# Row sums on ScalarE in place of VectorE's batch-norm statistics, in an attention and feed-forward kernel with hand-written orders

## The reference, cut to what matters

```
q   = layernorm(x)                      # over the 256 positions, eps 1e-5
kv  = k_i * v_j  (all channel pairs of a head, each position)
y   = causal convolution of kv with ssm_kernel[head]  + kv * D[head]
x   = x + sum_i y_ij * q_i
f   = layernorm(x)
x   = x + down( silu(gate(f)) * up(f) ) # HID = 704, weights are integers
```

## Time and profile before

| | |
|---|---|
| device time, median of 3 runs | 77.92 us (77.67 to 78.04) |
| span of the profiled execution, first to last instruction | 76.7 us |
| PE busy | 70.7 us, 92% |
| DVE busy | 63.9 us, 83% |
| POOL busy | 54.6 us, 71% |
| ACT busy | 46.7 us, 61% |
| chain that ended last, shares | PE 58%, DMA 15%, DVE 14%, ACT 3% |

### The profile page before, as it was taken

One profiled execution on the slowest core, in us unless ns is written; L12 is line 12 of the kernel. 1 busy time (PEld: TensorE's weight loads), 2 busy tenths in 40 slices (PEclk: granted clock), 3 DMA queues, 4 the chain that ended last, 5 costly groups with the idle time before them and its releaser, 6 DMA issues.

```text
span 76.7 us, 1495 instructions
## 1 busy us (share of the span) xinstructions
PE 70.7 (92%) x469; PEld 57.8 (75%) x469; DVE 63.9 (83%) x191; ACT 46.7 (61%) x115; POOL 54.6 (71%) x73
## 2 busy tenths in 40 slices
PE   4999988879999999999999999999999999999920
PEld 3767735568798777787888797988897989899810
DVE  0088399969999999899999999999999993786760
ACT  0601483275859587976868468746767798766400
POOL 5004798799889599299899949459627899939230
PEclk9999999999999999999999999999999999999995
DMA  0498999999997000000000000000000222200404
GB/s 5 132 256 279 386 344 295 285 384 397 386 353 220 13 0 0 0 0 4 4 9 0 0 0 0 0 0 0 0 9 4 68 68 68 68 9 0 137 0 137
DMA packets 7304, 8.29 MB, mean 108 GB/s; under 512 B 992, under 2 KB 6400, under 8 KB 7296
## 3 DMA queue, kind: packets, MB, share of 16 engines
q1 hardware_dynamic: 6912, 8.00, 31.7%
q10 hardware_dynamic: 384, 0.19, 0.8%
HBM read 7.12 MB, written 1.07 MB: 107 GB/s over the span
## 4 chain that ended last, share of the span: by engine, by line
PE 58%; DMA 15%; DVE 14%; SPq 3%; ACT 3%; issue 2%; DVEq 0%; ACTq 0%
PE conv L1010 18%; PE turn L957 8%; PE down L1029 8%; DMA k_ext<-ctx_ext 8%; DMA toeplitz<-taps 7%; PE conv L977 6%; PE conv L988 6%; PE conv L986 6%; DVE hidden L733 3%; DVE terms L718 2%; PE turn L939 2%; DVE terms L721 2%; PE turn L1029 2%; SPq L310 2%; ACT gate_act L508 1%
## 5 line engine op out<-in xcount | busy, mean ns | idle before, releaser
L1010 PE MATMUL conv<-f_parts,wgu 128*128 128x256 f16 x176 | 21.6, 273 | 0.3
L1010 PEld LDWEIGHTS conv<-f_parts,wgu 128*128 128x128 f16 x176 | 16.7, 98 | 3.5 <-DVE hidden L733 0.8
L376 POOL TENSOR_TENSOR products<-k_ext 128x512 f32<-128x512 f32 (+1 forms) x16 | 18.0, 1144 | 0.6 <-DMA k_ext<-ctx_ext 0.6
L508 ACT ACTIVATE gate_act<-conv,sg_sb 128x256 f32<-128x256 f32 (+1 forms) x24 | 11.2, 471 | 4.6 <-PE conv L1010 4.0
L258 POOL TENSOR_TENSOR h_lo<-hidden,h_hi 128x256 fp32r<-128x256 f32 x18 | 12.9, 729 | 1.4 <-ACT h_hi L513 1.3
L733 DVE SCALAR_TENSOR_TENSOR hidden<-conv,su_sb,gate_act 128x256 f32<-128x256 f32 (+1 forms) x24 | 11.3, 479 | 3.1 <-ACT gate_act L508 2.7
L977 PE MATMUL conv<-products,toeplitz 128*128 128x288 f32 x32 | 11.2, 434 | 0.3 <-DVE terms L725 0.3
L365 POOL TENSOR_TENSOR rstd_f<-variance_f,minus_half 128x1 f32<-128x1 f32 x8 | 5.5, 683 | 7.9 <-DVE variance_f L694 7.9
L718 DVE TENSOR_TENSOR terms<-conv,q_ext 128x512 f32<-128x512 f32 x16 | 10.8, 678 | 0.0
L986 PE MATMUL conv<-products,toeplitz 128*128 128x288 f32 x32 | 10.8, 422 | 0.0
L988 PE MATMUL conv<-products,toeplitz 128*128 128x288 f32 x32 | 10.4, 406 | 0.0
(11 more groups left out here) (64 smaller groups left out, 119.8 us busy)
## 6 DMA issues: line engine op xcount, KB each, us to landing
k_ext<-ctx_ext SPq DMA_DIRECT2D x3, 384.0 KB, 6.1
toeplitz<-taps_pad SPq DMA_DIRECT2D x2, 512.0 KB, 7.9
out<-x_sb SPq DMA_DIRECT2D x8, 128.0 KB, 1.7
toeplitz<-taps SPq DMA_DIRECT2D x3, 256.0 KB, 5.3
wg_int<-wg_t SPq DMA_DIRECT2D x1, 704.0 KB, 8.2
wu_int<-wu_t SPq DMA_DIRECT2D x1, 704.0 KB, 9.5
wd_int<-wd_t SPq DMA_DIRECT2D x1, 640.0 KB, 8.6
x_sb<-x SPq DMA_DIRECT2D x1, 512.0 KB, 7.0
```

The source lines that it names most:

```text
L376: nc.gpsimd.tensor_tensor(view(products[:, n:n + 1], first * MADE + GROUP, [[MADE, halves], [GROUP, 4], [1, GROUP]]), view(k, 0, [[EXT * B ...
L508: nc.scalar.activation(gate_act[up_lanes(t), i % 2, t, :], gate_of(i, t), ACT.Silu, scale=sg_sb[gate_lanes(t), t:t + 1]).then_inc(gate_act ...
L1010: done = nc.tensor.matmul(bank_of(i, t)[:, n, :], wgu[:, c, column:column + P], f_parts[:, i % 2, part, c, :], start=(c == 0 and part == 0 ...
```

## The change

For tiles 2 to 7, `stats_of_q` and `moments_of_q` on DVE go. ACT instead makes two passes over a tile's rows: `center_q` copies them scaled by -1/256 with the row sum in the accumulator output, which gives minus the mean; `spread_of_q` squares the rows plus that value, again with the row sum, which gives 256 times the variance. Their element-wise outputs go to `scratch`, which nobody reads. DVE turns two tiles' sums into variances in one operation (`variance_of_q_pair`), and POOL takes the power of both in one (`root_q_pair`), so that tiles 2/3, 4/5 and 6/7 share one of each. The shift multiplies minus the mean with the root.

The transfer of `skip` to all partitions goes: its 16 values stand in front of k's in DRAM and come with the first transfer of k. The small transfer of `skip_sb` goes too: D stands in the unused first column of `taps`. ACT issues two transfers where it issued four.

The four lists of POOL, ACT, DVE and PE are laid out anew over their whole length; SP's list keeps its order. The diff below is cut to the functions and to the lists' first part; behind it, operations of all kinds change places by a few positions.

```diff
+VECTOR_STATS = 2
...
-def build(nc, x, ctx_ext, taps, skip, wg_t, s_gate, wu_t, s_up, wd_t, s_down, taps_pad, out):
+def build(nc, x, ctx_skip, taps, wg_t, s_gate, wu_t, s_up, wd_t, s_down, taps_pad, out):
...
-k_ext = sb("k_ext", [P, H, HALVES, EXT * B])
+k_skip = sb("k_skip", [P, H + H * HALVES * EXT * B])
+skip_all = k_skip[:, 0:H]
+k_ext = k_skip[:, H:].rearrange("p (h c n) -> p h c n", h=H, c=HALVES)
...
-skip_sb = sb("skip_sb", [H, 1])
-skip_all = sb("skip_all", [P, H])
...
-minus_half = sb("minus_half", [P, 1])
+minus_half = sb("minus_half", [P, 2])
...
+minus_mean_q = sb("minus_mean_q", [P, TILES])
+spread_q = sb("spread_q", [P, TILES])
+scratch = sb("scratch", [P, 2, TILES, L])
...
     def load_k(first, last, done):
-        sp.dma_start(k_ext[:, first:last], ctx_ext[:, first:last]).then_inc(done, 16)
+        row = HALVES * EXT * B
+        columns = slice(H + first * row if first else 0, H + last * row)
+        sp.dma_start(k_skip[:, columns], ctx_skip[:, columns]).then_inc(done, 16)

...
     def root_q(t):
         wait(pool, q_variance, t + 1)
-        nc.gpsimd.tensor_tensor(rstd_q[:, t:t + 1], variance_q[:, t:t + 1], minus_half[:, :],
+        nc.gpsimd.tensor_tensor(rstd_q[:, t:t + 1], variance_q[:, t:t + 1], minus_half[:, 0:1],
                                 ALU.pow).then_inc(q_rstd, 1)
+
+    def root_q_pair(t):
+        wait(pool, q_pair_variance, (t - VECTOR_STATS) // 2 + 1)
+        nc.gpsimd.tensor_tensor(rstd_q[:, t:t + 2], variance_q[:, t:t + 2], minus_half[:, :],
+                                ALU.pow).then_inc(q_pair_rstd, 1)

     def root_f(t):
         wait(pool, f_variance, t + 1)
...
                                 ALU.pow).then_inc(f_rstd, 1)

     def add_skip_to_taps():
-        nc.gpsimd.tensor_tensor(taps_sb[:, P:P + 1], taps_sb[:, P:P + 1], skip_sb[:, :],
+        nc.gpsimd.tensor_tensor(taps_sb[:, P:P + 1], taps_sb[:, P:P + 1], taps_sb[:, 0:1],
                                 ALU.add).then_inc(taps_ready, 1)

...
                             base=0, pattern=[[-1, P]], channel_multiplier=1).then_inc(ident_ready, 1)
-    pool.wait_ge(taps_loaded, 32)
+    pool.wait_ge(taps_loaded, 16)
     add_skip_to_taps()
     pool.wait_ge(half_ready, 1)
     root_q(0)
     pool.wait_ge(k_loaded[2], 16)
     pairs(2, 0, 1)
+    root_q(1)
     pairs(2, 1, 2)
-    root_q(1)
     pairs(3, 0, 1)
     pairs(3, 1, 2)
+    root_q_pair(2)
     pool.wait_ge(k_loaded[3], 16)
     pairs(4, 0, 2)
-    root_q(2)
-    root_q(3)
     pairs(5, 0, 2)
     pairs(6, 0, 2)
     pairs(7, 0, 2)
+    root_q_pair(4)
+    merge_front(nc.gpsimd, 2)
+    root_f(0)
     pool.wait_ge(k_loaded[4], 16)
     pairs(8, 0, 2)
+    root_f(1)
     pairs(9, 0, 2)
-    merge_front(nc.gpsimd, 2)
-    root_q(4)
-    root_f(0)
-    root_q(5)
     pairs(10, 0, 2)
-    root_f(1)
+    merge_front(nc.gpsimd, 3)
+    root_q_pair(6)
     pairs(11, 0, 2)
-    root_q(6)
-    merge_front(nc.gpsimd, 3)
+    merge_front(nc.gpsimd, 4)
     pool.wait_ge(k_loaded[5], 16)
     pairs(12, 0, 2)
     root_f(2)
...
+    def center_q(t):
+        act.wait_ge(x_loaded[t // 2 + 1 if t < 4 else 3], 16)
+        nc.scalar.activation(scratch[:, 0, t, :], x_sb[:, t, :], ACT.Copy, scale=-1.0 / L,
+                             accum_out=minus_mean_q[:, t:t + 1]).then_inc(q_centered, 1)
+
+    def spread_of_q(t):
+        wait(act, q_centered, t + 1 - VECTOR_STATS)
+        nc.scalar.activation(scratch[:, 1, t, :], x_sb[:, t, :], ACT.Square, bias=minus_mean_q[:, t:t + 1],
+                             accum_out=spread_q[:, t:t + 1]).then_inc(q_spread, 1)
...
         act.wait_ge(wd_loaded, 3 * 16)
         convert(wd[:, :, :], wd_int[:, :, :]).then_inc(wd_ready, 1)

-    act.dma_start(skip_all[:, :], skip.rearrange("h a -> (h a)").partition_broadcast(P)).then_inc(skip_loaded, 16)
     act.dma_start(x_sb[:, 0, :], x[0:P, :]).then_inc(x_loaded[0], 16)
     act.dma_start(taps_sb[:, :], taps).then_inc(taps_loaded, 16)
-    act.dma_start(skip_sb[:, :], skip).then_inc(taps_loaded, 16)
     nc.scalar.preload_act_table(ACT.Silu)
     act.wait_ge(taps_ready, 1)
     act.dma_start(taps_pad, taps_sb[:, :]).then_inc(taps_stored, 16)
     norm_q(0)
+    evict_q(0)
     act.wait_ge(k_loaded[2], 16)
     squares(2)
-    evict_q(0)
+    center_q(2)
+    norm_q(1)
+    center_q(3)
     squares(3)
-    norm_q(1)
+    spread_of_q(2)
     act.wait_ge(k_loaded[3], 16)
     squares(4)
+    spread_of_q(3)
+    wrap(0)
+    evict_q(1)
     squares(5)
+    norm_q(2)
     squares(6)
+    evict_q(2)
+    wrap(1)
+    center_q(4)
+    center_q(5)
+    norm_q(3)
+    spread_of_q(4)
+    spread_of_q(5)
+    center_q(6)
+    center_q(7)
+    spread_of_q(6)
+    evict_q(3)
     squares(7)
-    evict_q(1)
     act.wait_ge(k_loaded[4], 16)
     squares(8)
-    norm_q(2)
-    wrap(0)
-    evict_q(2)
+    spread_of_q(7)
+    norm_q(4)
+    wrap(2)
+    convert_gate()
+    norm_q(5)
+    norm_f(0)
     squares(9)
-    wrap(1)
-    norm_q(3)
+    evict_q(4)
+    norm_f(1)
     squares(10)
-    convert_gate()
     squares(11)
-    wrap(2)
-    evict_q(3)
+    high_f(0)
+    wrap(3)
+    high_f(1)
+    convert_up()
     act.wait_ge(k_loaded[5], 16)
     squares(12)
-    convert_up()
-    norm_q(4)
...
+    def variance_of_q_pair(t):
+        wait(dve, q_spread, t + 2 - VECTOR_STATS)
+        dve.tensor_scalar(variance_q[:, t:t + 2], spread_q[:, t:t + 2], 1.0 / L, EPS, ALU.mult,
+                          ALU.add).then_inc(q_pair_variance, 1)
+
     def shift_of_q(t):
+        if t >= VECTOR_STATS:
+            wait(dve, q_pair_rstd, (t - VECTOR_STATS) // 2 + 1)
+            dve.tensor_scalar(shift_q[:, t:t + 1], minus_mean_q[:, t:t + 1], rstd_q[:, t:t + 1], None,
+                              ALU.mult).then_inc(q_shift, 1)
+            return
         wait(dve, q_rstd, t + 1)
         dve.tensor_scalar(shift_q[:, t:t + 1], moments_q[:, t, 0:1], rstd_q[:, t:t + 1], -1.0,
                           ALU.mult, ALU.mult).then_inc(q_shift, 1)
...
         dve.tensor_tensor(scaled_of(i, r), down_of(i, r), sd_sb[:, :], ALU.mult).then_inc(out_scaled, 1)

     dve.memset(zeros[:, :], 0.0).then_inc(zeros_ready, 1)
+    dve.wait_ge(x_loaded[0], 16)
+    stats_of_q(0)
     dve.wait_ge(k_loaded[0], 16)
     all_products(0, 0, 1)
+    moments_of_q(0)
...
     all_products(0, 1, 2)
+    variance_of_q(0)
     dve.wait_ge(anti_ready, 1)
-    dve.wait_ge(skip_loaded, 16)
     dve.wait_ge(direct_loaded[0], 16)
     direct(0)
-    dve.wait_ge(x_loaded[0], 16)
-    stats_of_q(0)
-    moments_of_q(0)
     dve.wait_ge(k_loaded[1], 16)
     all_products(1, 0, 1)
-    variance_of_q(0)
+    shift_of_q(0)
     dve.wait_ge(direct_loaded[1], 16)
     direct(1)
     all_products(1, 1, 2)
     dve.wait_ge(x_loaded[1], 16)
     stats_of_q(1)
-    shift_of_q(0)
     moments_of_q(1)
+    variance_of_q(1)
     dve.wait_ge(direct_loaded[2], 16)
     direct(2)
-    variance_of_q(1)
     direct(3)
-    dve.wait_ge(x_loaded[2], 16)
-    stats_of_q(2)
-    moments_of_q(2)
     shift_of_q(1)
     multiply_terms(0)
-    stats_of_q(3)
-    variance_of_q(2)
     multiply_terms(1)
-    moments_of_q(3)
+    variance_of_q_pair(2)
     dve.wait_ge(direct_loaded[3], 16)
     direct(4)
     direct(5)
-    variance_of_q(3)
+    shift_of_q(2)
+    multiply_terms(2)
+    multiply_terms(3)
+    add_sum(0)
+    stats_of_f(0)
+    shift_of_q(3)
+    multiply_terms(4)
     dve.wait_ge(direct_loaded[4], 16)
     direct(6)
-    shift_of_q(2)
-    multiply_terms(2)
-    dve.wait_ge(x_loaded[3], 16)
-    stats_of_q(4)
-    shift_of_q(3)
-    multiply_terms(3)
-    stats_of_q(5)
-    multiply_terms(4)
-    add_sum(0)
-    moments_of_q(4)
+    variance_of_q_pair(4)
     multiply_terms(5)
-    stats_of_q(6)
-    stats_of_f(0)
-    variance_of_q(4)
-    moments_of_q(5)
-    moments_of_q(6)
+    direct(7)
+    shift_of_q(4)
     moments_of_f(0)
-    variance_of_q(5)
     add_sum(1)
-    variance_of_q(6)
     variance_of_f(0)
+    variance_of_q_pair(6)
+    stats_of_f(1)
+    moments_of_f(1)
     merge_back(dve, 2)
-    direct(7)
-    stats_of_f(1)
-    stats_of_q(7)
-    shift_of_q(4)
+    variance_of_f(1)
+    shift_of_f(0)
+    shift_of_q(5)
     multiply_terms(6)
-    shift_of_f(0)
-    moments_of_f(1)
     add_sum(2)
-    variance_of_f(1)
+    shift_of_f(1)
     multiply_terms(7)
-    shift_of_q(5)
-    shift_of_f(1)
-    stats_of_f(2)
     low_f(0)
     multiply_terms(8)
     low_f(1)
...
     convolve_across(0)
     convolve_within(0)
     convolve_across(1)
-    convolve_within(1)
     pe.wait_ge(ident_ready, 1)
     turn_q(0, q_ready, 0)
+    convolve_within(1)
     convolve_across(2)
     convolve_within(2)
     turn_q(1, q_ready, 1)
     convolve_across(3)
     convolve_within(3)
+    sum_terms(0, q_ready, 0)
+    turn_q(2, q_ready, 2)
     convolve_across(4)
     convolve_within(4)
-    turn_q(2, q_ready, 2)
-    sum_terms(0, q_ready, 0)
     convolve_across(5)
     convolve_within(5)
+    turn_q(3, q_ready, 3)
+    sum_terms(1, x1_ready, 1)
```

(19 more changed lines are left out.)

213 lines of the change are left out of this document (102 added, 111 removed).

## The result

The changed kernel takes 79.98 us (median of 4 runs, 79.83 to 80.17) beside 77.98 (4 runs, 77.67 to 78.05) for the kernel before: a ratio of 1.027, 95% interval 1.024 to 1.031. It is slower by 2.0 us. The forecast was 76.9 with a range to 78.5; forecast and range are both wrong. The profiled execution took 80.06 with a span of 78.3.

A forecast was written before the change was run, and what follows sets the result against it. PE and DVE were taken as full in the late part, with holes early; 0.4 to 0.5 us early and 0.5 late cut the span to 75.7, plus 1.2 around it 76.9 us, range 75.8 to 78.5.

The forecast's parts named there:

- `sum_terms(2)` at 23.5 behind `merge_back(2)`: Replay to 26 us: PE reaches `sum_terms(2)` at 23.5, head 8 at 25.55, with a lead of 0.3 to 0.5 us.
- with the 1.2 us around it, 76.9 us: Final sum: a span of 75.7 us plus 1.2 us around it, set against the median of 77.92.
- The lead of 1.25 at head 5: Replay to 15 us: head 5 can start at 16.7 instead of 17.96 with the same work done, 1.25 us ahead.
- The late part, 0.5 gained on top of a lead of 0.4: After 33 us: DVE's lead of 0.7 and a full PE list close about half of PE's 1.2 us of holes.
- rival 2: Late part, DVE and PE both full: PE spends the early lead waiting for `hidden_units`; 77.8 us, chance 0.17.
- Transfers and skip weights at 0: Fewer ACT transfers and skip weights moved into another transfer: nothing gained, as what SP issues sooner queues.
- The start at 0: DVE takes `stats_of_q(0)` ahead of head 0's products; head 0 comes later, head 2 ends at 10.55 as before, cost 0.
- The price of the passes: Twelve ACT passes at 0.45 to 0.5 us per centre and 0.5 to 0.55 per spread, 6.1 us in all.
- rival 3: From 16.3 to 22.5 us ACT becomes the bound through its run of eight passes, so slower; 78.6 us, chance 0.18.
- DVE's 3.5: DVE loses six statistics at 0.419 and six aggregates at 0.172 us, 3.5 us less work.
- Rival 1: ACT's row sum costs nothing, each pass about 0.12 us cheaper; 76.1 us, chance 0.15.
- rival 4: At the start PE sits idle for 0.5 us and its clock rises later; 77.6 us, chance 0.05.

The follow-up runs named there:

- pairs_split: The changed kernel with POOL's `pairs(8)` and `pairs(11)` each made in two operations of half the length, in the same places; 78.67 us, ratio 1.008.
- skip_only: The kernel before with only the skip weights inside k's transfer and the two small ACT transfers gone; 78.16 us, ratio 1.004.
- f0_p8_early: The changed kernel with `multiply_terms(6)` behind `merge_back(2)`, `spread_of_q(7)` behind `wrap(2)`, later pairs halved, tile 0's second normalization and `pairs(8)` earlier; 79.04 us, ratio 1.017.

## Why the prediction was wrong

**The step that failed is "`sum_terms(2)` at 23.5 behind `merge_back(2)`".** I gave each operation of the replay its mean duration from the kernel before, whatever ran beside it. The step wanted the merge done in 0.7 us, but POOL's new list started `pairs(8)` 0.21 us before it. Measured: 1.61, and 1.73 for the next. Halving both POOL operations gave back 1.3 us; undoing the first alone 1.04, of which only 0.5 lies there. ACT was not what failed: `wrap(2)` was done at 22.38, the replay had it at 22.75. The kernel's text would have let me ask: DVE's merge and POOL's `pairs` both read SBUF with two inputs. The Trainium skill (SBUF — State Buffer, Summary: rules for kernel authors) says that a VectorE operation with two SBUF inputs and a GpSimd operation that reads SBUF exclude each other, and that the one that comes second waits for the whole of the first. The runs agree, in both directions (DVE 1.61 for 0.68, POOL 1.74 for 1.28), but for POOL's roots, which read SBUF too and held no merge (0.69 at most). With `pairs(8)` ending at 23.55 as measured, the rule puts the merge's end at 24.1 and `sum_terms(2)` at 24.2. It was a rival I did not name.

**The base.** The forecast's "with the 1.2 us around it, 76.9 us" mixed two executions. In the runs since, time minus span is 1.7 to 1.9, so the profiled execution of the kernel before took about 78.5 (76.7 and 1.8), 0.6 over its median, and it was one with late transfers (14.90 against 13.56 above). A replay that starts from it forecasts against 78.5, not 77.92: 0.6 us of error in the number. The lead of 1.25 at head 5 was partly that execution's own: 16.59 is 0.4 to 0.7 ahead of the 17.00 and 17.26 of the two other profiles.

**The late part, 0.5 gained on top of a lead of 0.4,** did not come. `pairs_split` is the fairest test, the changed kernel with its two longest waits shortened to 0.4 and 0.5. Head 8 started at 25.58 (forecast 25.55) and gates(0, 0) at 30.61 (30.5). At `hidden_units(2, 0)` it was 0.35 ahead of the kernel before; at the last one it was 0.13 behind (71.17 and 71.04) instead of 0.9 ahead. Between the two it lost the 0.6 of `low(1, 5)`. So the outcome is that of rival 2, to which I gave 0.17, but the lead did not go in small waits for `hidden_units`: it went in one more wait of the kind that I had not priced.

The sum: 76.9 forecast, 0.6 for the base, 1.3 for the two merges, 0.6 for `low(1, 5)`, and about 0.5 of lead that `pairs_split` lacks even so: 79.9, against 79.98. The last term is a remainder: what of it is ACT's passes, what the new orders and what the waits that are left, is open. Set against `skip_only`, a more typical run of the old orders, the changed kernel was 1.7 us behind at `hidden_units(2, 0)` and `pairs_split` 0.4: even with the waits shortened there was no early lead.

**What held.** Transfers and skip weights at 0: `skip_only`. The start at 0: head 3 at 11.41. The price of the passes: the row sum is an instruction of its own, as the timeline of the changed kernel shows at `center_q(4)` and `center_q(5)`,

```profile
16.59 0.40 ACT L485 ACTIVATE scratch<-x_sb 128x256 f32<-128x256 f32 x1
16.89 0.19 ACT L485 ACTIVATION_READ_ACCUMULATOR scratch<-x_sb 128x1 f32 x1
16.98 0.40 ACT L485 ACTIVATE scratch<-x_sb 128x256 f32<-128x256 f32 x1
```

and a centre comes every 0.40 us (forecast 0.45 to 0.5), a spread every 0.50. So rival 3 named a place where ACT was indeed full (5.76 of 6.00 us from 16 to 22, and `wrap(2)` held until 22.38), but a pass cost less than I took, and its way to a slower kernel is not the one that was measured. The paired root takes 0.71 us (taken 0.65). DVE's 3.5 was too high as well: successive operations overlap by 0.1, so six statistics and six aggregates free about 2.7 us. The waits within DVE's operations add up to 3.1 us in the changed kernel and 0.7 in the kernel before, which puts 2.4 back; the other 1.4 on the way to 1.1 busier lie in many small differences that I have not separated.

**Of the rivals,** number 3 had the right sign, by another mechanism, and with 78.6 was still 1.4 short. Rival 1 and rival 4 did not show: the row sum has its own instruction, and head 0 started at 4.80, head 2 at 8.81, no later than before (4.87, 9.07).

## What to carry to other kernels

When a list of DVE or POOL changes, lay the two timelines side by side and look for pairs of long operations that would overlap with both reading SBUF: the later one costs the rest of the earlier one. Look for ties too, two such operations that start at the same moment: `low(1, 5)` and `add(0, 1)` made 0.6 us of difference between versions that share that part of the list. Put operations that read PSUM there, or cut the long ones. Compare a profiled execution's own time with the median before resting a term on one hole of it; a hole that ends with a transfer may be that run's.

## What was not expected of the hardware

- POOL can take its turn twice: the DVE merge started at 31.17 waited for the operation that ran and for the next, 2.40 us in all.
- A single-input DVE operation of 128x2 waits (1.13, 1.24 us), while the same kind with 128x1 does not: in `skip_only` a variance of 128x1 took 0.13 at 21.16, inside POOL's `merge_front(2)`, and in `f0_p8_early`, `shift_of_f(0)` took 0.20 inside it. A batch-norm statistic, too, kept its 0.43. The timeline of the latter version:

```profile
21.36 0.43 DVE L729 BATCH_NORM_STATS2 stats_f<-x_sb 128x6 f32<-128x256 f32 x1
21.70 0.20 DVE L742 TENSOR_SCALAR shift_f<-moments_f,rstd_f 128x1 f32<-128x1 f32 x1
...
20.69 1.31 POOL L282 TENSOR_TENSOR terms<-terms 128x512 f32<-128x512 f32 x1
```
